# Moving the centering matmul behind the gate products in the projection step of a four-layer triangle kernel

## The chip, the cores and the metric

The kernel runs on one core of one Trainium2 chip. The metric is the device time of one execution in microseconds. Five engines work side by side, each through its own list of instructions in order: TensorE (PE; its weight loads are PEld), VectorE (DVE), ScalarE (ACT), GpSimd (POOL) and SyncE (SP), which issues the transfers. They wait for each other through counting semaphores.

## What is computed

The input `x` has 256 x 256 tokens of 64 channels. Four layers follow each other, and each adds its result to `x`:

```python
x = x + _L0_conv_ref(_gn(x), ...)
x = x + _L1_conv_ref(_gn(x), ...)
x = x + _L2_conv_ref(_gn(x), ...)
x = x + _L3_conv_ref(_gn(x), ...)
```

`_gn` is a group norm. Layers 0, 1 and 3 have one shape; this is layer 0, cut:

```python
xn = layernorm(x, norm_g, norm_b)
left = xn @ Wl.T * m * jax.nn.sigmoid(xn @ Wlg.T)
right = xn @ Wr.T * m * jax.nn.sigmoid(xn @ Wrg.T)
out_gate = jax.nn.sigmoid(xn @ Wog.T)
out = jnp.einsum('bikd,bjkd->bijd', left, right)
out = layernorm(out, out_norm_g, out_norm_b) * out_gate
return out @ Wout.T
```

Layer 3 has no mask `m`. Layer 2 has no layer norm ahead of its projections, and goes through another function.

## The kernel before

Each layer is done in three stages: the projections (everything up to `left`, `right` and `out_gate`, which go to DRAM), the product over `k`, and the output stage. The change is in the projections of layers 0, 1 and 3, in `project` (L418).

Tokens come in chunks of 512, two rows of the 256 x 256 image for each half of the image; the two halves lie on partitions 0 to 63 and 64 to 127. A layer has 64 chunks (`NCH`), and the main loop does one chunk a step, 16 steps (`BODY`) in one turn of a hardware loop. A step `q` works on several chunks at once, at distances that the line with `CENTER` sets:

```python
LOAD, CENTER, VARIANCE, SPLIT, NORM = 16, 14, 13, 5, 4
```

On TensorE a step issues these products, in an order written out by hand in `step` (L573):

- `spread` for chunk q+4 (L549), which puts 1/sqrt(variance) on all partitions,
- `center` for chunk q+14 (L530), a float32 product that takes the mean away and writes the one bank `Z`,
- `heads` for chunk q, row 0 and row 1 (L562), 24 small float16 products. Row 0 writes `PAIR[0]` and row 1 writes `PAIR[1]`. There is one such buffer a row,
- `out_gate` for chunk q (L569 to L571), three float16 products into the bank `GATE`,
- `variance` for chunk q+13 (L541), a float32 product that adds up squares of eight chunks in the bank `VAR`.

`center` and `variance` stop before the others: the last 14 steps of a layer have no `center`, the last 13 no `variance`.

ScalarE does in each step, in this order: `square` for chunk q+14 (L606, L608), two passes over `Z` that store the centred values (`zs`) and their squares (`sq`); `gate_pair` for chunk q, row 0 and row 1 (L625), the sigmoids of the halves of `PAIR[0]` and `PAIR[1]`; in one step of eight also `root` (L613 to L618), a logarithm and an exponential with table loads around them; and the sigmoid of `GATE` (L642), written to `gates`.

VectorE does `norm` for chunk q+4 (L692, L693, L699), which makes the float16 parts `hi` and `lo` that `heads` reads four steps later, and `left_and_right` for chunk q (L712), which multiplies the other half of `PAIR[0]`, then of `PAIR[1]`, by its sigmoids. That is the last read of the pair buffer. In layers 0 and 1 GpSimd then multiplies by the mask (L745, L759). In layer 3 L712 writes `stage` itself.

These waits hold the step together:

```python
pe.wait_ge(pair_read.sem, pair_read(m * 2 + row - 1))      # heads, row of chunk m
pe.wait_ge(c["gate_done"].sem, c["gate_done"](m))          # out_gate
pe.wait_ge(c["sq_done"].sem, c["sq_done"](readers))        # center
act.wait_ge(c["z_done"].sem, c["z_done"](m + 1))           # square
```

The first says that `heads` of a row may start once L712 has read the same row of the chunk before. The third says that `center` may overwrite `Z` once the squares of the chunk before are made.

Of the kernel before, what the change touches and what calls it, by code (L numbers as in the profile page):

```python
# [41 lines left out]
BODY = 2 * SCH  # L42
# [151 lines left out]
class Fold:  # L194
# [42 lines left out]
    def load(self, sp):  # L237
        for dst, src in self.loads:
            sp.dma_start(dst, src).then_inc(self.loaded.sem, 16)
# [178 lines left out]
def project(nc, n, kind, low, HG, x, a, left_right, c, k, ps):  # L418
# [8 lines left out]
    LOAD, CENTER, VARIANCE, SPLIT, NORM = 16, 14, 13, 5, 4  # L427
    masked, gate = kind != "normed", a["gate"]
    with ExitStack() as ctx:
# [31 lines left out]
        def bodies_of(eng, step):  # L461

            with eng.Fori(0, bodies - 1) as i:
                for q in range(BODY):
                    step(i, q, lambda lead: True)
            for q in range(BODY):
                step(bodies - 1, q, lambda lead: q + lead < BODY)
# [54 lines left out]
        @block.tensor  # L522
        def _(pe):
            def center(i, q, bank, readers):

                m = i * BODY + q
                load = c[f"x_in{q % 8 // 2}"]
                pe.wait_ge(load.sem, load(i * 32 + (q // 8 + 1) * 16))
                pe.wait_ge(c["sq_done"].sem, c["sq_done"](readers))
                pe.matmul(bank, k["center"][:], xs[:, q % 8, :], start=True, stop=True).then_inc(c["z_done"].sem, 1)  # L530

            def variance(i, q):

                m = i * BODY + q
                pe.wait_ge(c["sq_done"].sem, c["sq_done"](m + 1))
                at = q % BATCH
                if at == 0:
                    batch = i * (BODY // BATCH) + q // BATCH
                    pe.wait_ge(c["log_done"].sem, c["log_done"](batch))
                w = k["var_w"][:, 2 * (BATCH - 1 - at):2 * (2 * BATCH - 1 - at)]  # L540
                pe.matmul(VAR, w, sq[:, q % 2, :], start=(at == 0), stop=(at == BATCH - 1)).then_inc(c["var_done"].sem, 1)  # L541

            def spread(i, q):

                m = i * BODY + q
                b = q // BATCH
                pe.wait_ge(c["r_split"].sem, c["r_split"](i * (BODY // BATCH) + b + 1))
                pe.wait_ge(c["xn_done"].sem, c["xn_done"](m))
                pe.matmul(R, k["spread"][:, q % BATCH, :], r_terms[:, b % 2, :], start=True, stop=True).then_inc(c["spread_done"].sem, 1)  # L549

            def heads(i, q, row):
                m = i * BODY + q
                if row == 0:
                    pe.wait_ge(c["lo_done"].sem, c["lo_done"](m + 1))

                pe.wait_ge(pair_read.sem, pair_read(m * 2 + row - 1))
                for kb in range(2):
                    at = row * S + kb * P
                    for step, (tokens, part) in enumerate(((hi, 0), (lo, 0), (hi, 1))):
                        for g in range(2):  # L560
                            half = slice(g * C, g * C + C)
                            last = pe.matmul(PAIR[row][:, g, kb * S:kb * S + S], tokens[half, q % 8, at:at + P],  # L562
                                             k["w_heads"][half, part, :], start=(step == 0), stop=(step == 2))
                last.then_inc(c["proj_done"].sem, 1)

            def out_gate(i, q):
                m = i * BODY + q
                pe.wait_ge(c["gate_done"].sem, c["gate_done"](m))
                pe.matmul(GATE, k["w_gate"][:, 0, :], hi[:, q % 8, :], start=True, stop=False)  # L569
                pe.matmul(GATE, k["w_gate"][:, 0, :], lo[:, q % 8, :], start=False, stop=False)  # L570
                pe.matmul(GATE, k["w_gate"][:, 1, :], hi[:, q % 8, :], start=False, stop=True).then_inc(c["gate_mm_done"].sem, 1)  # L571

            def step(i, q, more):  # L573
                if more(NORM):
                    spread(i, q + NORM)
                if more(CENTER):
                    center(i, q + CENTER, Z, i * BODY + q + CENTER)
                heads(i, q, 0)
                heads(i, q, 1)
                out_gate(i, q)  # L580
                if more(VARIANCE):
                    variance(i, q + VARIANCE)

            fold.multiply_statistics(pe)
            pe.wait_ge(fold.done.sem, fold.done(8))

            between = {0: (fold.multiply_bias, fold.center_output), 1: (fold.multiply_weights,), 4: (fold.turn_sizes,),
                       5: (fold.spread_sizes,)}
            for q in range(CENTER):
                center(0, q, AHEAD_Z[q % 2], q - 1)  # L590
                if q > 0:
                    variance(0, q - 1)
                for part in between.get(q, ()):
                    part(pe)
                if q >= CENTER - NORM:
                    spread(0, q - (CENTER - NORM))
            pe.wait_ge(fold.done.sem, fold.done(fold.all_steps))
            bodies_of(pe, step)

        @block.scalar  # L600
# [918 lines left out]
```

## Time and profile before

| | |
|---|---|
| median of 3 runs | 2241.92 us |
| all three | 2240.76, 2241.92, 2245.84 us |
| profiled execution, device time | 2241.74 us |
| its span, first to last instruction | 2239.9 us |
| mean granted TensorE clock | 0.948 |
| PE busy | 1814.5 us (81%) |
| DVE busy | 1521.0 us (68%) |
| ACT busy | 1309.4 us (58%) |
| POOL busy | 807.1 us (36%) |

The device time is 1.8 us above the span of the same execution. Busy shares are means over stages with different limits, so a stage is read by itself. The main loops of the projections lie at about 97 to 372 us (layer 0), 720 to 995 us (layer 1) and 1631 to 1908 us (layer 3). Starts of instructions on one engine tell its pace; matmul records overlap each other, so their durations are not added up.

### The profile page before, as it was taken

The page shows a single profiled execution, that of the slowest core. Times are in us where ns is not written, and L with a number is a line of the kernel's source. Part 1 is how long each engine was busy: PE and PEld are TensorE (multiplying, and loading weights), DVE is VectorE, ACT ScalarE, POOL GpSimd, SP SyncE. Part 2 cuts the span into 40 slices and gives each one's busy share as a digit, 9 for nine tenths or more (in the row PEclk, how much of TensorE's full clock was granted, in tenths as well). Part 3 has the DMA queues.
Part 4 walks back from the last instruction along what each step waited for, and adds up shares of the span by engine and source line. Part 5 has one row for each costly group of instructions (what it writes and reads, how often), then busy time and mean ns, then how long its engine had stood idle before and what let it go on. Part 6 is the DMA issues. An engine that isn't in the chain of part 4 may idle for free. (4 is left out here: it accounts for less than half of the span.)

```text
span 2239.9 us, 40644 instructions
## 1 busy us (share of the span) xinstructions
PE 1814.5 (81%) x10389; PEld 966.6 (43%) x10389; DVE 1521.0 (68%) x3171; ACT 1309.4 (58%) x2413; POOL 807.1 (36%) x740
## 2 busy tenths in 40 slices
PE   0999994897998999955699786777799998499766
PEld 0333442784542344333355464633233434388432
DVE  7588885226745999966875575488488889244675
ACT  0577773466995777744599464333377776144322
POOL 0144444006960444444798000088100000000699
PEclk9999998898999999988899899899899999699999
DMA  7368677775993454547499698399547767655699
GB/s 318 111 189 256 207 240 231 283 293 199 366 335 117 154 183 159 169 142 300 155 366 361 216 305 287 158 365 399 200 127 231 238 212 224 237 230 220 210 352 338
DMA packets 353472, 542.22 MB, mean 242 GB/s; under 512 B 23627, under 2 KB 205518, under 8 KB 345686
## 3 DMA queue, kind: packets, MB, share of 16 engines
q1 hardware_dynamic: 353366, 541.01, 70.1%
q8 instruction: 41, 0.67, 0.1%
q14 instruction: 65, 0.53, 0.1%
HBM read 314.43 MB, written 226.49 MB: 241 GB/s over the span
## 5 line engine op out<-in xcount | busy, mean ns | idle before, releaser
L1263 POOL TENSOR_TENSOR out_scaled<-O,out_rs 128x128 f32<-128x128 f32 (+1 forms) x128 | 97.9, 767 | 739.0 <-DVE out_rs L1170 737.8
L562 PE MATMUL ps<-w_heads,hi 64*128 64x256 f16 x3072 | 292.1, 273 | 29.0 <-DVE sig L712 20.1
L1059 ACT ACTIVATE O<-ps 128x512 f32 (+1 forms) x144 | 151.8, 1054 | 233.4 <-PE ps L979 233.4
L625 ACT ACTIVATE sig<-ps,largest 128x512 f32<-128x512 f32 x384 | 246.5, 691 | 51.4 <-PE ps L562 49.9
L606 ACT ACTIVATE zs<-ps,shift 128x512 f32<-128x512 f32 x192 | 131.7, 686 | 213.3 <-PE ps L530 209.7
L1307 PE MATMUL ps<-ident,out_scaled 128*128 128x128 f32 (+1 forms) x1024 | 163.8, 285 | 107.6 <-POOL out_scaled L1263 107.5
L1307 PEld LDWEIGHTS ps<-ident,out_scaled 128*128 128x128 f32 (+1 forms) x1024 | 114.7, 134 | 278.1 <-POOL out_scaled L1263 193.7
L562 PEld LDWEIGHTS ps<-w_heads,hi 64*128 64x128 f16 x3072 | 154.3, 95 | 181.3 <-issue 65.9
L1004 DVE COPY packed<-right 128x512 f32<-128x512 f32 (+1 forms) x208 | 96.9, 490 | 190.4 <-DMA right<-left_right 141.0
L745 POOL TENSOR_TENSOR stage<-sig,mask 128x512 f32<-128x512 f32 x128 | 133.4, 1076 | 236.2 <-DVE sig L712 236.2
L979 PE MATMUL ps<-left,packed 128*128 128x256 f32 (+1 forms) x768 | 154.7, 355 | 77.8 <-DVE packed L1004 77.0
L562 PE MATMUL ps<-w_heads,lo 64*128 64x256 f16 x1536 | 213.2, 272 | 0.0
L712 DVE SCALAR_TENSOR_TENSOR sig<-ps,largest,sig 128x512 f32<-128x512 f32 x256 | 179.8, 742 | 44.4 <-ACT sig L625 43.0
L759 POOL TENSOR_TENSOR stage<-sig,mask 128x1024 bf16<-128x1024 f32 x64 | 130.4, 2038 | 210.4 <-DVE sig L712 210.4
L530 PE MATMUL ps<-xs,center 128*128 128x512 f32 x384 | 204.6, 615 | 1.1 <-DVE shift L336 1.1
L541 PE MATMUL ps<-sq,var_w 128*16 128x512 f32 x384 | 200.0, 603 | 4.3 <-ACT log_var L615 4.3
L1162 DVE BATCH_NORM_STATS2 out_bn<-O 128x6 f32 (+2 forms) x1024 | 193.8, 255 | 12.5 <-PEq L921 12.3
L1249 POOL TENSOR_TENSOR out_centered<-O,out_bn 128x512 f32<-128x512 f32 x128 | 134.7, 1053 | 149.0 <-DVE out_bn L1162 149.0
L699 DVE TENSOR_TENSOR lo<-xn,hi 128x512 f16<-128x512 f32 x192 | 180.4, 939 | 6.6
L1274 POOL TENSOR_TENSOR out_xo<-out_og,out_xs 128x512 f32<-128x512 f32 x128 | 168.0, 1315 | 28.1 <-DMA x_dram<-out_xo 15.5
L979 PEld LDWEIGHTS ps<-left,packed 128*128 128x128 f32 (+1 forms) x768 | 120.7, 163 | 112.1 <-issue 60.9
L1349 ACT ACTIVATE out_u<-ps 32x512 f32<-32x512 f32 (+1 forms) x128 | 75.5, 590 | 154.1 <-PE ps L1307 154.1
(136 smaller groups left out, 3645.2 us busy)
## 6 DMA issues: line engine op xcount, KB each, us to landing
left_right<-stage SPq DMA_DIRECT2D x128, 512.0 KB, 6.4
out_gs<-gate SPq DMA_DIRECT2D x256, 256.0 KB, 4.5
gate<-gates SPq DMA_DIRECT2D x96, 512.0 KB, 2.9
x_dram<-out_xo SPq DMA_DIRECT2D x192, 256.0 KB, 4.3
out_xs<-x_dram SPq DMA_DIRECT2D x192, 256.0 KB, 4.6
left<-left_right SPq DMA_DIRECT2D x22, 2048.0 KB, 7.8
right<-left_right SPq DMA_DIRECT2D x22, 2048.0 KB, 12.2
xs<-x_dram SPq DMA_DIRECT2D x64, 512.0 KB, 4.1
```

What stands on the lines that cost most here:

```text
L530: pe.matmul(bank, k["center"][:], xs[:, q % 8, :], start=True, stop=True).then_inc(c["z_done"].sem, 1)
L541: pe.matmul(VAR, w, sq[:, q % 2, :], start=(at == 0), stop=(at == BATCH - 1)).then_inc(c["var_done"].sem, 1)
L562: last = pe.matmul(PAIR[row][:, g, kb * S:kb * S + S], tokens[half, q % 8, at:at + P], k["w_heads"][half, part, :], start=(step == 0), sto ...
L625: act.activation(sig[:, slot, :].rearrange("p (c e) -> p c e", c=4), pair(row, 0), ACT.Sigmoid, scale=k["largest"][:, 0:1]).then_inc(c["si ...
L699: dve.tensor_tensor(lo[:, q % 8, :], xn[:, q % 2, :], hi[:, q % 8, :], ALU.subtract).then_inc(c["lo_done"].sem, 1)
L712: dve.scalar_tensor_tensor(dst, pair(row, 1).rearrange("p c (n h) -> p c n h", h=HG), k["largest"][:, 1:2], factor, ALU.mult, ALU.mult).th ...
L979: last = pe.matmul(ps[h % 4 // 2][:, h % 2, jb * S:jb * S + S], stationary, moving, start=(kb == 0), stop=(kb == 1))
L1059: act.activation(o_of(ch), ps[h % 4 // 2][:, h % 2, :].rearrange("p (b g i) -> p b g i", b=2, g=2), ACT.Copy).then_inc(c["o_copied"].sem, 1)
L1162: last = dve.bn_stats(bn[:, b, jb, at:at + 2, :].rearrange("p g s -> p (g s)"), tokens.rearrange("p g h -> p h g"))
L1249: pool.tensor_tensor(centered[:, q % RING], rows[:, :, bass.ds(m * 2 * ROWS, 2 * ROWS), :], per_token(bn[:, :, :, :, 1:2], q), ALU.subtrac ...
L1274: pool.tensor_tensor(xo[:, q % RING, :], og[:, q % RING], xs[:, q % RING, :], ALU.add).then_inc(c["x_new"].sem, 1)
L1307: last = pe.transpose(TURNED[q % 4][:, at:at + P], scaled[:, q % RING, jb, 2 * row:2 * row + 2, :].rearrange("p g h -> p (g h)"), k["ident ...
```

## The change

In a step of the main loop, `center` goes from ahead of `heads` to behind `out_gate`. A wait for `sq_done` with the same target as the one inside `center` is put ahead of `out_gate`. The prologue, which centres the first 14 chunks, is not changed, nor is any other engine's list.

```diff
             def step(i, q, more):
                 if more(NORM):
                     spread(i, q + NORM)
+                heads(i, q, 0)
+                heads(i, q, 1)
+                if more(CENTER):
+                    pe.wait_ge(c["sq_done"].sem, c["sq_done"](i * BODY + q + CENTER))
+                out_gate(i, q)
                 if more(CENTER):
                     center(i, q + CENTER, Z, i * BODY + q + CENTER)
-                heads(i, q, 0)
-                heads(i, q, 1)
-                out_gate(i, q)
                 if more(VARIANCE):
                     variance(i, q + VARIANCE)
```

Two places of the order show it. First TensorE, from the variance product of one step to the first `heads` product of the next. Names in brackets are the semaphores waited for. Before:

```order
L541 MATMUL ps<-sq,var_w 16x512 [waits sq_done]
L548 REGISTER_ALU [waits r_split]
L549 MATMUL ps<-r_terms,spread 128x512 [waits xn_done]
L529 REGISTER_ALU [waits x_in1]
L530 MATMUL ps<-xs,center 128x512 [waits sq_done]
L556 ISA [waits lo_done]
L562 MATMUL ps<-w_heads,hi 128x256 [waits pair_read]
```

The same engine after the change, from the gate products of one step to the first `heads` product of the next:

```order
L569 MATMUL ps<-hi,w_gate 128x512 [waits gate_done,sq_done]
L570 MATMUL ps<-lo,w_gate 128x512
L571 MATMUL ps<-hi,w_gate 128x512
L530 MATMUL ps<-xs,center 128x512 [waits sq_done,x_in1]
L541 MATMUL ps<-sq,var_w 16x512 [waits sq_done]
L548 REGISTER_ALU [waits r_split]
L549 MATMUL ps<-r_terms,spread 128x512 [waits xn_done]
L556 ISA [waits lo_done]
L562 MATMUL ps<-w_heads,hi 128x256 [waits pair_read]
```

The centre product of chunk q+14 now stands behind the gate products of chunk q, and between it and the `heads` of chunk q+1 stand the variance and the spread product. Before, the next products behind the centre were the `heads` of the same step.

Second ScalarE, one step after the change (its line numbers are two higher than before, as two lines were added above):

```order
L608 ACTIVATE zs<-ps,shift 128x512 [waits xn_done,z_done]
L610 ACTIVATE sq<-ps,shift 128x512 [waits var_done]
L625 ISA
L626 REGISTER_ALU [waits proj_done]
L627 ACTIVATE sig<-ps,largest 128x512 [waits lr_done]
L625 REGISTER_ALU
L626 REGISTER_ALU [waits proj_done]
L627 ACTIVATE sig<-ps,largest 128x512 [waits lr_done]
```

Nothing moved here: the two passes over the centre product still stand ahead of the sigmoids of the same step.

## Rows read from the trace of the kernel before

**Rows 1.** The page's busy shares: busy us, share of the span, instructions.

```profile
PE 1814.5 (81%) x10389; PEld 966.6 (43%) x10389; DVE 1521.0 (68%) x3171; ACT 1309.4 (58%) x2413; POOL 807.1 (36%) x740
```

**Rows 2.** Windows: stretch, its length, busy us by engine, PEclk, DMA share, GB/s.

```profile
120.00:140.00 20.00, 20.00 (x157) 8.51 (x155) 16.03 (x24) 14.01 (x24) 9.90 (x10) 1.00 0.53 169
340.00:360.00 20.00, 14.00 (x166) 8.96 (x166) 18.75 (x28) 11.54 (x18) 12.34 (x12) 1.00 0.73 214
962.00:970.00 8.00, 4.77 (x58) 2.92 (x56) 7.93 (x11) 3.92 (x7) 3.93 (x3) 1.00 0.22 88
1880.00:1900.00 20.00, 14.44 (x158) 7.67 (x158) 18.63 (x25) 11.65 (x18) 0.00 (x0) 1.00 0.93 271
```

**Rows 3.** Timeline, one steady step of layer 0: start us, duration us, instruction.

```profile
204.47 0.39 PE L549 MATMUL ps<-r_terms,spread 128*128 128x512 bf16 x1
...
204.69 1.02 PE L530 MATMUL ps<-xs,center 128*128 128x512 f32 x2
...
205.65 0.28 PE L562 MATMUL ps<-w_heads,hi 64*128 64x256 f16 x2
...
205.75 0.69 ACT L606 ACTIVATE zs<-ps,shift 128x512 f32<-128x512 f32 x1 [1.31 <-PE ps L530]
...
206.91 1.26 ACT L625 ACTIVATE sig<-ps,largest 128x512 f32<-128x512 f32 x2
...
207.06 0.39 PE L569 MATMUL ps<-hi,w_gate 128*128 128x512 f16 x1
...
207.63 1.41 DVE L712 SCALAR_TENSOR_TENSOR sig<-ps,largest,sig 128x512 f32<-128x512 f32 x2 [0.72 <-ACT sig L625]
...
207.81 1.03 PE L541 MATMUL ps<-sq,var_w 128*16 128x512 f32 x2
208.05 0.70 ACT L642 ACTIVATE gates<-ps,largest 128x512 f32<-128x512 f32 x1
...
208.78 0.39 PE L549 MATMUL ps<-r_terms,spread 128*128 128x512 bf16 x1
```

**Rows 4.** Timeline, a step of layer 0 without centre and variance.

```profile
343.35 1.40 DVE L712 SCALAR_TENSOR_TENSOR sig<-ps,largest,sig 128x512 f32<-128x512 f32 x2
...
344.24 0.29 PE L562 MATMUL ps<-w_heads,hi 64*128 64x256 f16 x2 [0.98 <-DVE sig L712]
...
345.65 0.39 PE L569 MATMUL ps<-hi,w_gate 128*128 128x512 f16 x1
```

**Rows 5.** Timeline, the same of layer 3.

```profile
1887.71 1.98 DVE L712 SCALAR_TENSOR_TENSOR stage<-ps,largest,sig 128x512 f32<-128x512 f32 x2
...
1890.51 0.39 PE L569 MATMUL ps<-hi,w_gate 128*128 128x512 f16 x1
```

**Rows 6.** Timeline, a step with the root in layer 0, and the next root.

```profile
143.45 1.26 ACT L625 ACTIVATE sig<-ps,largest 128x512 f32<-128x512 f32 x2
...
144.73 1.28 ACT L613 ACT_TABLE_LOAD   x1
...
148.76 0.69 ACT L642 ACTIVATE gates<-ps,largest 128x512 f32<-128x512 f32 x1
...
149.50 0.39 PE L569 MATMUL ps<-hi,w_gate 128*128 128x512 f16 x1 [1.52 <-ACT gates L642]
...
180.81 1.28 ACT L613 ACT_TABLE_LOAD   x1
```

**Rows 7.** Line L625 by itself: its table loads (ns: min, median, max).

```profile
L625 ACT ACT_TABLE_LOAD  x3: 1283/1283/1283, 99.0 to 1632.7; - x3
```

**Rows 8.** Timeline, the root step without a centre in layer 0.

```profile
328.41 0.39 PE L569 MATMUL ps<-hi,w_gate 128*128 128x512 f16 x1 [1.98 <-ACT gates L642]
...
329.62 0.61 PE L549 MATMUL ps<-r_terms,spread 128*128 128x512 bf16 x1 [0.39 <-DVE r_terms L677]
```

**Rows 9.** Windows of one us at both kinds of root step.

```profile
148.00:149.00 1.00, 0.00 (x0) 0.00 (x0) 0.93 (x3) 0.99 (x2) 0.00 (x0) 1.00 1.09 324
...
331.00:332.00 1.00, 1.00 (x14) 0.81 (x12) 1.00 (x3) 0.01 (x1) 1.00 (x2) 0.50 1.09 364
```

## The prediction

> **What bounds the kernel now.** I read the page first: TensorE is busy 81% of the span, more than any other engine [rows 1], but that is a mean over twelve stages. So I cut out the stage that the change touches. In the main loop of the projections TensorE is busy all of a 20 us window at full granted clock (1.00, the 2.4 GHz level), while VectorE has 16.03 us and ScalarE 14.01 us of work [rows 2]. The timeline of one step shows how it is packed. From spread to spread are 4.31 us (204.47 to 208.78), and TensorE starts something new all the time: spread 0.22 us, centre 0.96, heads 1.41, gate products 0.75, variance 0.97 [rows 3]. ScalarE keeps up: it stands idle 1.31 us before each pass over the centre product. It waits for TensorE, not TensorE for it. One step in eight holds the root, and there TensorE waits 1.52 us for the gate sigmoid; eight steps take 36.08 us (144.73 to 180.81) where eight plain ones would take 34.5 [rows 6].
>
> So a step costs what TensorE's instructions cost, and every wait on another engine is covered by other products. The question is whether it stays covered.
>
> **The chain that the change closes.** ScalarE works in order, and its list is not changed: the two passes over centre q+14 come ahead of the sigmoids of chunk q. VectorE's product of row 0 needs the first sigmoid, and the heads of chunk q+1 need that product, since there is one pair buffer a row. Before, the centre was issued ahead of heads q, so the passes ran under heads q. Now the centre comes behind the gate products of chunk q, so heads q+1 wait for: centre, two passes, sigmoid, product. Only variance and spread lie beside that. It is a ring, centre to centre, and its length is:
>
> - centre start to first pass: 204.69 to 205.75, 1.06 us [rows 3]
> - first pass to first sigmoid: 205.75 to 206.91, 1.16 us [rows 3]
> - first sigmoid to VectorE's product: 206.91 to 207.63, 0.72 us [rows 3]
> - product to first heads of the next chunk, where heads wait for it: 343.35 to 344.24, 0.89 us [rows 4]
> - heads to gate products: 344.24 to 345.65, 1.41 us [rows 4]
> - gate products to what follows: 207.06 to 207.81, 0.75 us [rows 3]. What follows was the variance; now it is the centre, whose weights are larger. The three gate products alone take 0.65, so 0.65 to about 0.85 is possible. I take 0.75, from the row where a float32 product follows the same three.
>
> Sum **5.99 us a step** against 4.31. TensorE's own instructions still take 4.31, so it stands idle 1.7 us in each step: variance and spread end their issue 2.15 us after the centre starts (0.96 + 0.97 + 0.22), and the heads may start at 3.83. In layer 1 the product has the same shape. In layer 3 both products are longer, and from the first product to the gate products there are 2.80 us (1887.71 to 1890.51, [rows 5]) in place of 0.89 + 1.41. That makes **6.49 us**.
>
> Not on the ring: the gate sigmoid of chunk q starts 1.14 us after the first sigmoid and takes 0.70 [rows 3], so it is done 4.1 us after the centre, before the next gate products need it at 5.24. VectorE's norm of the next chunk fits between the second product and the next first one; its work, 16.03 us in 20 us or 3.5 us a step, is well under 5.99. The added wait for `sq_done` asks for the squares of chunk q+13, made in the step before; it costs nothing, since those squares stand ahead of the sigmoids that heads waited for. If it were late, the gate products and all behind them would be too, but it cannot be later than the product that released the heads. Loads, stores and GpSimd get the same instructions over a longer time: the transfers take 0.53 of the engines in the first window [rows 2]. They cost nothing more.
>
> **The root steps.** Here the gate sigmoid ends the wait. From the first sigmoid to the gate products of the next step are 6.05 us (143.45 to 149.50, [rows 6]), which holds two table loads, the logarithm and the exponential. The variance that the root reads is done 2 us after the centre, before the root starts. Centre to centre: 1.06 + 1.16 + 6.05 + 0.75 = **9.02 us**, in all three layers. Before, such a step took 4.31 + 1.52 = 5.8.
>
> **The sum.** A layer has 64 - 14 = 50 steps with a centre, so 49 intervals from centre to centre, 6 of them with a root. Before: 6 x 36.08 + 4.31 = 220.8 us. After, layers 0 and 1: 43 x 5.99 + 6 x 9.02 = 311.7; layer 3: 43 x 6.49 + 6 x 9.02 = 333.2. To that come the ends: the first centre starts 1.41 + 0.75 later than before, and from the last centre to the next heads there are 3.83 us in place of 4.31, together +1.7; and the table load for the first sigmoid, 1.28 us [rows 7], was beside TensorE's work and now is in the ring, +1.3. So layers 0 and 1: 311.7 - 220.8 + 3.0 = +94 each; layer 3: 333.2 - 220.8 + 3.0 = +115. **Together +303 us.** The 14 steps behind them are as before.
>
> **The clock** is the term with no row of its own. In a new root step TensorE stands idle from the end of heads (5.2 us, with the tail of the last product 5.3) to the gate products at 8.3, near 2.9 us. What rows show: an idle of 1.52 us in the root steps before leaves the granted clock at 1.00 [rows 6, 9]. In the root step without a centre TensorE stood idle 1.98 us, then again 0.39 us, and the spread product behind it took 0.61 in place of 0.39 us; the clock was 0.50, the 1.2 GHz level [rows 8, 9]. The gap of 2.9 us is on the far side of both, so I take it that the clock falls after each of the 18 roots. Then the parts of the ring that TensorE does are doubled for a while: centre about +1.0, part of the gate products +0.3, and, if it lasts that long, heads +1.4. Bounds 0 (it never falls) and 1.06 + 0.75 + 1.41 = 3.2 us; I take 2.0, nearer the second row. 18 x 2.0 = **+36 us**. In plain steps the idle is 1.7 us of 5.99. The stretches without a centre have the same pattern (TensorE busy 14.00 of 20 us, 4.77 of 8, 14.44 of 20, an idle gap in each step), and their clock is 1.00 [rows 2], so I expect no fall there.
>
> Total +303 + 36 = +339 us on the profiled execution's 2241.7, which stands 0.2 us under the median of the runs: **2581 us**.
>
> The Trainium skill, Perfetto Trace Analysis, section Matmuls, says that independent groups should rotate through PSUM banks, so that ScalarE's and VectorE's reading of one lies under the next group's products. By that rule alone, with rows 0 and 1 in two buffers and `Z` and `GATE` in two more, the move would cost nothing, and the sum would be 0. The 0.98 us that the heads wait in each step without a centre [rows 4] speaks against it: two buffers that are both needed again in the next step don't cover the reading.
>
> **The rivals.**
>
> *The clock falls in every turn.* The new idle comes back in each step, and the third layer's is longer, near 1.9 us (heads may start at 4.16, after 2.15 of issue and a tail of 0.1). If this holds the clock at the lower level, the TensorE parts of the ring double: +3.2 us a step. In layer 3 alone that is 50 x 3.2 = +160, 2740 us; in all three +480, about 3060 us. For it: 1.98 + 0.39 us idle was enough once [rows 8]. Against: the windows at 1.00 with gaps of the same kind [rows 2]. [...] Chance 10%.
>
> *The cover holds, no change* (2242 us). Variance and spread would have to hide passes, sigmoid and product. They give 2.15 us, and 3.83 are wanted; it decides at 1.7 us less of either. Chance 3%.
>
> *Faster, through the root stall.* Heads now stand directly behind spread, 0.96 us earlier in the step. If the sigmoids started that much earlier, the gate sigmoid behind each root would too, and up to 0.96 us of each 1.52 us stall [rows 6] would go: 18 x 0.96 = 17 us, 2224 us. It decides at whether ScalarE can start sigmoid q before centre q+14 is there. Its list says no: the pass stands ahead, and waits. Chance 2%.
>
> **How the numbers follow.** The forecast, with its own bounds, gets 85%. Low end: no fall of the clock and 0.65 for the hand-over, 303 - 15 = +288, 2530 us. High end: 18 x 3.2 = +58 for the roots, 303 + 58 = +361, 2603 us; and I add +47 for layer 3 at the low clock in some 15 of its 50 steps (15 x 3.2), 2650 us. The range 2530 to 2650 leaves out most of the first rival and the two small ones. A measurement of this kernel can tell a change of about 0.2% from none. Slower by more than that has 95%, no change 3%, faster 2%.
>
> **What would show it.** Starts of the centre product 5.99 us apart in layers 0 and 1 and 6.49 in layer 3, 9 to 11 at a root; ScalarE's first pass with its idle before it grown from 1.31 to about 3 us; heads with some 1.5 us idle before them, released by L714 (the product's new line); gate products waiting for the gate sigmoid only at the root; 18 dips of the granted clock to 0.50. The prediction is wrong if heads show no wait in steady steps, if the plain step is not within 0.2 us of these lengths, or if the clock is down in plain steps.

## The result and the profile after

| | before | after |
|---|---|---|
| median | 2241.34 us (4 runs) | 2574.57 us (4 runs) |
| ratio to before, 95% interval | | 1.1481 [1.1463, 1.1499] |
| profiled execution, device time | 2241.74 us | 2567.97 us |
| its span | 2239.9 us | 2566.2 us |

One run after (7906.1 us) and one run of e11 (4708.87 us) were in a slow state and take no part in any ratio; the median of the other three after is 2572.74 us. That is 331.4 us above the median before; 2581 was forecast, between 2530 and 2650. The profiled executions lie 326.3 us apart in span. All line numbers behind the TensorE step are two higher than before, so the product L712 is L714 here and the first pass L606 is L608.

The page after: busy shares, and the granted clock by fortieths of the span.

```profile
PE 1855.1 (72%) x10305; PEld 985.6 (38%) x10389; DVE 1533.2 (60%) x3171; ACT 1311.1 (51%) x2413; POOL 806.4 (31%) x740
...
PEclk9999999798999999997999898998989898989999
...
L562 PE MATMUL ps<-w_heads,hi 64*128 64x256 f16 x3072 | 314.7, 283 | 295.4 <-DVE sig L714 183.6
L608 ACT ACTIVATE zs<-ps,shift 128x512 f32<-128x512 f32 x192 | 131.9, 687 | 537.3 <-PE ps L530 537.3
```

TensorE's share is down from 81% to 72% [rows 1]: the same work in a longer time. The idle ahead of the heads is 295.4 us in all, and nearly all of it ends with VectorE's product (`sig` in layers 0 and 1, `stage` in layer 3). The page before gave 29.0 us for that group. ScalarE waits 537.3 us for the centre product, where it was 213.3.

A steady step of layer 0 after the change, from the timeline (start us, duration us, instruction, idle before it and who ended it). It answers to [rows 3].

```profile
209.69 1.02 PE L530 MATMUL ps<-xs,center 128*128 128x512 f32 x2
210.64 1.03 PE L541 MATMUL ps<-sq,var_w 128*16 128x512 f32 x2
210.75 0.69 ACT L608 ACTIVATE zs<-ps,shift 128x512 f32<-128x512 f32 x1 [2.83 <-PE ps L530]
...
211.91 1.27 ACT L627 ACTIVATE sig<-ps,largest 128x512 f32<-128x512 f32 x2
212.63 1.41 DVE L714 SCALAR_TENSOR_TENSOR sig<-ps,largest,sig 128x512 f32<-128x512 f32 x2 [2.23 <-ACT sig L627]
...
213.44 0.28 PE L562 MATMUL ps<-w_heads,hi 64*128 64x256 f16 x2 [1.76 <-DVE sig L714]
...
214.86 0.39 PE L569 MATMUL ps<-hi,w_gate 128*128 128x512 f16 x1
...
215.52 1.02 PE L530 MATMUL ps<-xs,center 128*128 128x512 f32 x2
```

Centre to centre is 5.83 us in this step. The ring can be read off link by link: centre to first pass 1.06, to the sigmoid 1.16, to the product 0.72, to the next heads 0.81, to the gate products 1.42, to the centre 0.66.

One of these rows has to be read with care. The spread product stands between the variance product and the heads in every step, but its matmul record is missing from this trace in 84 of 192 steps, this one among them (its weight load is there each time, and the page has 84 matmuls fewer than the one before). So the 1.76 us at 213.44 hold 0.32 us of work. Where the record is there, TensorE's idle in a plain step is 1.44 us, as at 219.26 below; in e2, e5 and e8, which keep this ring and lose no such record, it is 1.44 us in nearly every plain step of layers 0 and 1. The spread line by itself after the change (ns: min, median, max, then the first and last start in us):

```profile
L549 PEld LDWEIGHTS ps<-r_terms,spread x192: 95/96/152, 87.9 to 2216.1; 128*128 128x128 bf16 x192
L549 PE MATMUL ps<-r_terms,spread x108: 379/390/634, 90.0 to 2216.4; 128*128 128x512 bf16 x108
```

The step with the root, and the clock behind it: first the timeline, TensorE and the gate sigmoid (it answers to [rows 6]), then windows of one us with the columns of [rows 2].

```profile
219.26 0.28 PE L562 MATMUL ps<-w_heads,hi 64*128 64x256 f16 x2 [1.44 <-DVE sig L714]
...
222.96 0.69 ACT L644 ACTIVATE gates<-ps,largest 128x512 f32<-128x512 f32 x1
...
223.79 0.59 PE L569 MATMUL ps<-hi,w_gate 128*128 128x512 f16 x1 [3.04 <-ACT gates L644]
...
225.03 1.91 PE L530 MATMUL ps<-xs,center 128*128 128x512 f32 x2
```

```profile
222.00:223.00 1.00, 0.00 (x0) 0.00 (x0) 0.96 (x2) 0.99 (x2) 0.00 (x0) 0.88 1.14 340
223.00:224.00 1.00, 0.21 (x1) 0.13 (x2) 0.92 (x4) 0.65 (x1) 0.00 (x0) 0.50 1.06 310
...
228.00:229.00 1.00, 0.76 (x1) 0.10 (x1) 0.07 (x1) 1.00 (x3) 0.00 (x0) 0.50 0.00 0
229.00:230.00 1.00, 0.26 (x6) 0.24 (x8) 1.00 (x2) 1.00 (x2) 0.14 (x1) 0.71 0.00 0
```

TensorE stands idle 3.04 us, the clock falls to 0.50 (1.2 GHz) before the wait is over, and the centre takes 1.91 us in place of 1.02. The windows put the fall at 222.8 and the return at 229.6, 6.8 us later. The same wait does not always end so: in layers 0 and 1 it is 3.04 to 3.12 us at each of twelve roots, and the clock fell at ten of them.

Layer 3 has the same in steps without a root. The timeline shows two plain steps of it, and the windows the clock under the first.

```profile
1914.42 0.28 PE L562 MATMUL ps<-w_heads,hi 64*128 64x256 f16 x2 [1.77 <-DVE stage L714]
...
1916.33 0.61 PE L569 MATMUL ps<-hi,w_gate 128*128 128x512 f16 x1
...
1922.45 0.30 PE L562 MATMUL ps<-w_heads,hi 64*128 64x256 f16 x2 [2.09 <-DVE stage L714]
...
1925.03 0.61 PE L569 MATMUL ps<-hi,w_gate 128*128 128x512 f16 x1
```

```profile
1914.00:1915.00 1.00, 0.58 (x12) 0.50 (x12) 1.00 (x2) 0.40 (x1) 0.00 (x0) 1.00 0.00 0
1915.00:1916.00 1.00, 0.92 (x18) 0.55 (x12) 0.97 (x3) 0.00 (x0) 0.00 (x0) 0.88 0.00 0
1916.00:1917.00 1.00, 1.00 (x6) 0.28 (x3) 0.94 (x2) 0.00 (x0) 0.00 (x0) 0.50 0.00 0
...
1920.00:1921.00 1.00, 0.37 (x1) 0.10 (x1) 0.00 (x0) 1.00 (x3) 0.00 (x0) 1.00 0.04 8
```

Here the heads wait 1.77 us in a step (the 2.09 at 1922.45 hold a spread product whose record is missing), and with a short gap ahead of row 1 TensorE is idle 1.85 us of 6.41. The clock falls in 14 of 43 plain steps.

Read off the starts of ScalarE's first pass, from the one for chunk 14 to the one for chunk 63 in each layer (49 intervals):

| | before | after | plain interval | six root intervals |
|---|---|---|---|---|
| layer 0 | 220.5 us | 313.9 us | 5.82 us | 60.4 us in all, 5 of 6 with a fall of the clock |
| layer 1 | 221.3 | 313.6 | 5.82 | 59.9, 5 of 6 |
| layer 3 | 222.3 | 357.3 | 6.41, but 14 of 43 at 7.75 to 8.13 | 57.9, 3 of 6 |

The growth is 93.4 + 92.4 + 135.0 = 320.8 us of the 326.3 between the two spans. The other 5.5 us lie before, between and behind these stretches, where 5.1 us were forecast for the ends of the loops. Nothing large outside the three loops has to be explained.

### The profile page after: what moved, and what is told of

Same layout as the page of the kernel before. It is cut to its first block and busy times, and to the rows that moved or that the text cites. A ratio compares the mean times of both kernels' runs of the same rounds, so it can differ in the third digit from the quotient of the medians.

```text
span 2566.2 us, 40836 instructions
## 1 busy us (share of the span) xinstructions
PE 1855.1 (72%) x10305; PEld 985.6 (38%) x10389; DVE 1533.2 (60%) x3171; ACT 1311.1 (51%) x2413; POOL 806.4 (31%) x740
## 5 line engine op out<-in xcount | busy, mean ns | idle before, releaser
L562 PE MATMUL ps<-w_heads,hi 64*128 64x256 f16 x3072 | 314.7, 283 | 295.4 <-DVE sig L714 183.6
L608 ACT ACTIVATE zs<-ps,shift 128x512 f32<-128x512 f32 x192 | 131.9, 687 | 537.3 <-PE ps L530 537.3
L1265 POOL TENSOR_TENSOR out_scaled<-O,out_rs 128x128 f32<-128x128 f32 (+1 forms) x128 | 91.7, 718 | 874.4 <-DVE out_rs L1172 873.3
L714 DVE SCALAR_TENSOR_TENSOR sig<-ps,largest,sig 128x512 f32<-128x512 f32 x256 | 180.4, 746 | 235.5 <-ACT sig L627 235.5
L562 PEld LDWEIGHTS ps<-w_heads,hi 64*128 64x128 f16 x3072 | 159.8, 97 | 369.3 <-DVE sig L714 161.0
L714 DVE SCALAR_TENSOR_TENSOR stage<-ps,largest,sig 128x512 f32<-128x512 f32 x128 | 127.6, 1073 | 164.7 <-ACT sig L627 164.7
L530 PE MATMUL ps<-xs,center 128*128 128x512 f32 x384 | 220.0, 657 | 2.3 <-ACT sq L610 1.3
L562 PE MATMUL ps<-w_heads,lo 64*128 64x256 f16 x1536 | 221.4, 281 | 0.0
L701 DVE TENSOR_TENSOR lo<-xn,hi 128x512 f16<-128x512 f32 x192 | 194.4, 1013 | 6.6
L1276 POOL TENSOR_TENSOR out_xo<-out_og,out_xs 128x512 f32<-128x512 f32 x128 | 161.7, 1264 | 28.6 <-DMA x_dram<-out_xo 16.1
```

Of the source, the lines that this page charges most:

```text
L701: dve.tensor_tensor(lo[:, q % 8, :], xn[:, q % 2, :], hi[:, q % 8, :], ALU.subtract).then_inc(c["lo_done"].sem, 1)
L714: dve.scalar_tensor_tensor(dst, pair(row, 1).rearrange("p c (n h) -> p c n h", h=HG), k["largest"][:, 1:2], factor, ALU.mult, ALU.mult).th ...
L1276: pool.tensor_tensor(xo[:, q % RING, :], og[:, q % RING], xs[:, q % RING, :], ALU.add).then_inc(c["x_new"].sem, 1)
```

## The experiments

The theory: the change closes a ring (centre, two passes, sigmoid, product, heads, gate products, centre), because ScalarE's passes stand ahead of the sigmoids of the same step and each row has one pair buffer. Its length sets the step, and the idle in it brings the clock down now and then. The rival: the new place itself is dear on TensorE, by the added wait, by weights that are not loaded ahead, or by the clock alone.

**e1: open the ring on ScalarE.** TensorE's order is that of the change.

```diff
             def step(i, q, more):
                 m = i * BODY + q
-                if more(CENTER):
-                    square(i, q + CENTER, Z)
                 gate_pair(i, q, 0)
                 gate_pair(i, q, 1)
                 root_step(i, q, more)
...
                 act.activation(gates[:, q % 4, :], GATE, ACT.Sigmoid, scale=k["largest"][:, 2:3]).then_inc(c["gate_done"].sem, 1)
+                if more(CENTER):
+                    square(i, q + CENTER, Z)
```

> TensorE as in the change; only ScalarE's list is altered: the two passes over the centre product come last in a step, behind the gate sigmoid. Ring theory: the sigmoids of chunk q no longer stand behind the centre of the same step, so the ring is open and the plain step goes back to TensorE's own 4.31 us; at a root the passes come late and the step may be some 0.7 us longer than the 5.8 of before. In all 2235 to 2265 us. Rival theory (the centre behind the gate products is dear on TensorE itself, by its weights or by the added wait): nothing changes, about 2570 us.

Measured: 2273.13 us, ratio 1.0141 [1.0117, 1.0165]. Of the 331 us some 300 are gone with TensorE's list untouched, so the place of the centre is not dear in itself. But it came out 8 us above the range. The timeline of a root in e1:

```profile
151.65 0.69 ACT L642 ACTIVATE gates<-ps,largest 128x512 f32<-128x512 f32 x1
152.23 0.68 ACT L608 ACTIVATE zs<-ps,shift 128x512 f32<-128x512 f32 x1
...
152.80 0.69 ACT L610 ACTIVATE sq<-ps,shift 128x512 f32<-128x512 f32 x1
...
153.55 0.39 PE L569 MATMUL ps<-hi,w_gate 128*128 128x512 f16 x1 [2.93 <-ACT sq L610]
```

The gate products now wait for the squares behind the root: the added wait for `sq_done`, which costs nothing in the change, decides here. TensorE stands idle 2.93 us in place of 1.52, 1.4 us more at each of 18 roots, 25 us. The clock also fell at seven of the 18, where in the kernel before it fell at none.

**e2: the added wait only once.** The prologue reads chunk 13 in the bank `GATE`, so the first gate products need the wait. The later ones don't.

```diff
-                if more(CENTER):
-                    pe.wait_ge(c["sq_done"].sem, c["sq_done"](i * BODY + q + CENTER))
                 out_gate(i, q)
...
             pe.wait_ge(fold.done.sem, fold.done(fold.all_steps))
+            pe.wait_ge(c["sq_done"].sem, c["sq_done"](CENTER))
             bodies_of(pe, step)
```

> The change, but the wait for sq_done ahead of the gate products stands once ahead of the main loop and not in each step. Ring theory: it never ended a wait, so the time stays at that of the change, within 0.3% of 2572 us, and the plain step at 5.82 us. Rival theory (the wait holds up TensorE in each step, some 0.1 to 0.2 us): 15 to 30 us less. A third: with its own wait the centre's weights are not loaded ahead, and the plain step grows from 5.82 by up to 0.2 us, 30 us more.

Measured: 2572.77 us, ratio to before 1.1485 [1.1465, 1.1504], the change's being 1.1481. The plain interval is 5.82 and 6.41 us as in the change. The wait costs nothing there, as forecast, and neither rival to that is seen. As this is the same ring a second time, it also shows how the falls of the clock repeat: at 12 of 18 roots and in 15 of 43 plain steps of layer 3, against 13 and 14 in the change.

**e3 and e4: shorten the ring from its TensorE end.** In e3 the centre stands between heads and gate products, in e4 between the two rows of heads; the added wait is left out of both.

First e3:

```diff
                 heads(i, q, 0)
                 heads(i, q, 1)
                 if more(CENTER):
-                    pe.wait_ge(c["sq_done"].sem, c["sq_done"](i * BODY + q + CENTER))
-                out_gate(i, q)
-                if more(CENTER):
                     center(i, q + CENTER, Z, i * BODY + q + CENTER)
+                out_gate(i, q)
```

then e4:

```diff
                 heads(i, q, 0)
-                heads(i, q, 1)
                 if more(CENTER):
-                    pe.wait_ge(c["sq_done"].sem, c["sq_done"](i * BODY + q + CENTER))
-                out_gate(i, q)
-                if more(CENTER):
                     center(i, q + CENTER, Z, i * BODY + q + CENTER)
+                heads(i, q, 1)
+                out_gate(i, q)
```

> The centre between heads and the gate products. Ring theory: the ring loses the 0.66 us of the gate products, so 5.16 us a plain step in layers 0 and 1 and 5.75 in layer 3; the root interval goes back to 7.0 us, since the centre no longer waits for the gate sigmoid; no fall of the clock. From centre to centre 43 x 5.16 + 6 x 7.0 = 264 in place of 220.8 us, layer 3 289; in all +155, about 2400 us. Rival (the position alone is dear, not the length of the ring): as the change, 2570, or as before, 2241.

> The centre between heads row 0 and heads row 1. Ring theory: 1.06 + 1.16 + 0.72 + 0.81 + 0.70 = 4.45 us a plain step in layers 0 and 1, 0.33 more in layer 3 (4.78), a hair above TensorE's own 4.31; root interval 7.0. In all about +53, 2295 us. Rival (any centre behind a heads product costs the whole): near 2400 or 2570 us.

Measured: e3 2426.74 us, ratio 1.083 [1.0808, 1.0851]; e4 2324.4 us, ratio 1.0373 [1.035, 1.0396]. Plain intervals of ScalarE's first pass are 5.27 and 5.85 us (layer 3) in e3, and 4.62 and 4.95 in e4, where 5.16, 5.75, 4.45 and 4.78 were expected. The intervals follow the length of the ring, each 0.10 to 0.17 longer than its sum.

Both totals came out above what was expected, by 27 us in e3 (about 2400) and 29 us in e4 (2295). The longer plain steps make 14 and 22 us of that. The first interval of each layer, which the expectations had left out, is 1.4 us longer than a plain one, and 2.7 to 2.9 in two layers of e3: 7 and 4 us. And "no fall of the clock" did not hold in e3: behind six of its roots a step is 1.1 us longer with the clock down, behind two in e4.

For the 0.10 the timeline of e4 has a reason:

```profile
204.50 0.30 PEld L530 LDWEIGHTS ps<-xs,center 128*128 128x128 f32 x2 [0.21 <-issue]
204.51 1.12 PE L530 MATMUL ps<-xs,center 128*128 128x512 f32 x2
...
205.67 0.69 ACT L606 ACTIVATE zs<-ps,shift 128x512 f32<-128x512 f32 x1 [1.61 <-PE ps L530]
```

and the change beside it:

```profile
215.30 0.41 PEld L530 LDWEIGHTS ps<-xs,center 128*128 128x128 f32 x2
215.52 1.02 PE L530 MATMUL ps<-xs,center 128*128 128x512 f32 x2
...
216.58 0.69 ACT L608 ACTIVATE zs<-ps,shift 128x512 f32<-128x512 f32 x1 [2.82 <-PE ps L530]
```

Behind a long gate product the centre's weights are loaded 0.22 us ahead. Behind the small heads products the load is recorded together with the matmul, and the centre lasts 1.12 in place of 1.02 us. So there the centre costs 0.10 more, and ScalarE starts 1.16 in place of 1.06 us after it. It is the same in most steps: 172 of 192 centre products last 1.12 to 1.13 us in e3 and 174 in e4. That the late load is the reason is read from this pattern; a load made to come earlier was not tried. The other 0.07 us in e4 lies between VectorE's product and the centre (1.57 us for 1.51).

**e10: shorten the ring from its ScalarE end.** Only the squares stay ahead of the sigmoids; the other pass comes behind them.

```diff
                 if more(CENTER):
-                    square(i, q + CENTER, Z)
+                    n = i * BODY + q + CENTER
+                    act.wait_ge(c["z_done"].sem, c["z_done"](n + 1))
+                    act.wait_ge(c["var_done"].sem, c["var_done"](n - 1))
+                    act.activation(sq[:, (q + CENTER) % 2, :], Z, ACT.Square, bias=k["shift"][:])
                 gate_pair(i, q, 0)
                 gate_pair(i, q, 1)
+                if more(CENTER):
+                    act.wait_ge(c["xn_done"].sem, c["xn_done"](n - 15))
+                    act.activation(zs[:, (q + CENTER) % 16, :], Z, ACT.Identity, bias=k["shift"][:]).then_inc(c["sq_done"].sem, 1)
```

> The change, but of ScalarE's two passes only the squares stay ahead of the sigmoids; the pass that stores the centred values comes behind them and signals for both. Ring theory: one pass of 0.58 us leaves the ring, so plain steps 5.24 us in layers 0 and 1 and 5.83 in layer 3, root intervals still 9.0 to 10.5. 3 x 43 x 0.58 = 75 us less than the change, and up to 20 more where the shorter idle in layer 3 keeps the clock up: 2477 to 2500 us. Rival (not the length of the ring but the place of the centre sets the time): 2572 us.

Measured: 2475.16 us, ratio 1.1049 [1.1031, 1.1066], with the median of the centre-to-centre intervals 5.25 us in layers 0 and 1 and 5.84 in layer 3. TensorE's list is that of the change. A pass of 0.58 us taken out of the ring takes 0.57 us off every plain step. In layer 3 TensorE is now idle 1.28 us in a plain step, and the clock falls in none of them. The total is 2 us below the expected range of 2477 to 2500: 74 us from the shorter steps and the 21 us of falls in layer 3 make 95 of the 98 us. Shortened from TensorE's side or from ScalarE's, the step follows the sum of the links. A second pair buffer would be the third way to open the ring; it wasn't tried, since all eight banks of PSUM are in use.

**e5 and e8: does the idle bring the clock down, and what does that cost?** Both give TensorE work that changes no value, in a wait that stays. In e5 the row 1 products behind each root are issued four times in a row, in e8 the spread product of layer 3. First e5:

```diff
-                for kb in range(2):
+                for kb in [kb for turn in range(4 if row == 1 and q % BATCH == 3 else 1) for kb in range(2)]:
```

then e8:

```diff
+                for turn in range(3 if kind == "normed" else 0):
+                    pe.matmul(R, k["spread"][:, q % BATCH, :], r_terms[:, b % 2, :], start=True, stop=True)
                 pe.matmul(R, k["spread"][:, q % BATCH, :], r_terms[:, b % 2, :], start=True, stop=True).then_inc(c["spread_done"].sem, 1)
```

> The change, with the twelve heads products of row 1 issued four times in a row (the same values) in the step behind each root, so that TensorE works 2 us of the 2.9 us in which it waits for the gate sigmoid. The work fits in the wait and lies off the ring. If the idle before the gate products is what lets the clock fall there, the 12 to 13 root intervals of 9.6 to 10.5 us come back to 9.0 and the time falls by 16 to 18 us, to about 2556 us, with the clock at 1.00 in the root steps; the falls in plain steps of layer 3 stay. Rival (the clock falls for another reason, or the falls cost nothing): 2572 or more.

> The change, with the spread product of layer 3 issued four times in a row (the same values), so that TensorE's idle ahead of the heads in a plain step of layer 3 falls from 1.9 to 1.25 us; the heads can't start earlier or later for it. If that idle is what makes the clock fall in 15 plain steps of layer 3 (7.8 to 8.1 us in place of 6.41), all plain steps of layer 3 are 6.41 and the time falls by some 20 us, to about 2552 us. Rival (the idle does not decide): 2572 us or, if the added products were on the ring, up to 64 x 0.66 = 42 us more.

Measured: e5 2557.15 us, ratio 1.1403 [1.1385, 1.142]; e8 2552.92 us, ratio 1.1377 [1.1359, 1.1394]. Against the change's 2572.74 that is 16 and 20 us less (17 and 23 by the ratios), and neither interval touches the change's. More work, less time. In e5 the gate products stand as follows:

```profile
221.31 0.38 PE L569 MATMUL ps<-hi,w_gate 128*128 128x512 f16 x1 [1.08 <-ACT gates L644]
...
221.96 1.02 PE L530 MATMUL ps<-xs,center 128*128 128x512 f32 x2
```

The idle is 1.08 in place of 3.04 us, the centre 1.02 us long. All twelve root intervals of layers 0 and 1 are 8.92 to 9.00 us. In layer 3 one of six is still 10.04, and the clock falls in 17 of its 43 plain steps, where it was 14. In e8 every plain interval of layer 3 but the first is 6.40 to 6.49 us, with an idle of 1.20 us in place of 1.85; the clock there still falls at three of six roots. A window of 260 us over layer 3's loop, first the change, then e8:

```profile
1900.00:2160.00 260.00, 179.88 (x1112) 72.83 (x1128) 139.04 (x201) 123.97 (x196) 0.00 (x0) 0.90 0.45 139
```

```profile
1900.00:2160.00 260.00, 201.80 (x1333) 77.67 (x1332) 149.92 (x216) 133.85 (x210) 0.00 (x0) 0.99 0.48 150
```

The clock's mean rises from 0.90 to 0.99.

**e6, e9, e11, e12: is there a better order?** Each root held up the gate products for 1.52 us in the kernel before. e6 keeps the change's TensorE order and ScalarE does sigmoids, gate sigmoid, passes, root. e9 is the kernel before with one step moved:

```diff
                 gate_pair(i, q, 0)
                 gate_pair(i, q, 1)
-                root_step(i, q, more)
...
                 act.activation(gates[:, q % 4, :], GATE, ACT.Sigmoid, scale=k["largest"][:, 2:3]).then_inc(c["gate_done"].sem, 1)
+                root_step(i, q, more)
```

> TensorE as in the change; ScalarE does sigmoids, gate sigmoid, the two passes over the centre product, and last the root. In e1 the gate products waited at each root for the squares behind the root (2.93 us idle in place of 1.52). Here the squares come ahead of the root, so plain steps 4.31 us and a stall of about 1.2 us a root, at the heads, released by the product: 2232 to 2242 us. If the order of the passes were not the cause of e1's 30 us: about 2270 us.

> The kernel before, TensorE's order untouched; only the root on ScalarE goes behind the gate sigmoid of its step. The gate products of the next step then need not wait for the root, and the passes and sigmoids of the next step come about 8.2 us after the step's start, with the heads wanting the product only at 9.8: stall 0 to 0.3 in place of 1.52 us at each root. 18 to 21 roots x 1.3 to 1.5 = 23 to 32 us less than before, 2209 to 2218 us. Rival (the stall only moves to the heads): 2236 to 2241 us.

Measured: e6 2265.36 us, ratio 1.0098 [1.0083, 1.0114]: 8 us under e1, but not under before, and 23 us above the expected range. Plain steps are 4.31 us, so the ring is open. What is left sits at the roots, in the timeline of e6:

```profile
152.13 0.39 PE L549 MATMUL ps<-r_terms,spread 128*128 128x512 bf16 x1 [1.55 <-DVE r_terms L679]
...
153.03 0.28 PE L562 MATMUL ps<-w_heads,hi 64*128 64x256 f16 x2 [0.50 <-DVE sig L714]
```

I had reckoned with the heads' wait alone and overlooked the spread product's: the root now ends later, and VectorE splits its result in 2.6 us before the spread may read it. The two waits are 2.05 us in place of 1.52, which makes 10 us at 18 roots. The clock also fell behind eight of the 18 roots, and the step there is some 1.5 us longer: 12 us more.

e9 measured 2236.54 us, ratio 0.9981 [0.9971, 0.9991]. It is the fastest kernel here, though by 0.2% only, where more than 1% was expected. The stall moved, as the rival had it, and its place in the timeline of e9 is not the heads but the spread product. The idle is 1.11 us in place of 1.52:

```profile
149.96 0.39 PE L549 MATMUL ps<-r_terms,spread 128*128 128x512 bf16 x1 [1.11 <-DVE r_terms L677]
...
150.34 1.41 DVE L712 SCALAR_TENSOR_TENSOR sig<-ps,largest,sig 128x512 f32<-128x512 f32 x2 [0.45 <-ACT sig L625]
```

e11 and e12 are e9 with more room for the split; both edits are shown against e9. First e11:

```diff
-    LOAD, CENTER, VARIANCE, SPLIT, NORM = 16, 14, 13, 5, 4
+    LOAD, CENTER, VARIANCE, SPLIT, NORM = 16, 14, 13, 4, 3
```

then e12:

```diff
-    LOAD, CENTER, VARIANCE, SPLIT, NORM = 16, 14, 13, 5, 4
+    LOAD, CENTER, VARIANCE, SPLIT, NORM = 16, 14, 13, 5, 3
```

> e9 with the spread product and norm three chunks ahead in place of four and the split one step later, so that the spread no longer waits for the split behind a root (1.11 us idle in e9). If that wait was all that was left of the stall: 18 x 1.1 = 20 us less than e9, about 2217 us. If the heads wait for the late sigmoids by the same amount, as the timeline of e9 suggests (product done 1.2 us after the heads' turn): within 4 us of e9, 2233 to 2241 us.

> e9 with the spread product and norm three chunks ahead in place of four, but the split left where it was in VectorE's list. In e11 the split had come to stand right ahead of the product and the spread that wait for it (2.15 us idle), beside 1.05 us at the heads. Here the first wait should go and the second stay: about 1.05 us a root at the heads, released by the product, none at the spread. Against e9 (1.11 us at the spread): the same within 0.3%, 2230 to 2240 us. If the heads' wait were only an echo of the split: 2215 to 2220 us.

e11 measured 2294.14 us (median of five runs), ratio 1.0242 [1.0226, 1.0257], worse than either branch of its expectation. Its timeline shows a wait at the heads and, in the step behind it, the wait at the spread product, grown from 1.11 to 2.15 us:

```profile
194.49 0.28 PE L562 MATMUL ps<-w_heads,hi 64*128 64x256 f16 x2 [1.05 <-DVE sig L712]
...
199.85 0.39 PE L549 MATMUL ps<-r_terms,spread 128*128 128x512 bf16 x1 [2.15 <-DVE r_terms L677]
```

The split had been moved with the spread, and in VectorE's list it now stood right ahead of a product that the heads want. In layer 1 the spread waits even longer, 2.7 to 2.8 us, and the clock fell at five of the 18 roots. e12 leaves it in its place: 2239.42 us, ratio 0.9991 [0.9979, 1.0003], no change against before. The spread's wait is gone, the heads' 1.05 us is there:

```profile
186.31 0.28 PE L562 MATMUL ps<-w_heads,hi 64*128 64x256 f16 x2 [1.05 <-DVE sig L712]
```

Its trace lacks records of the spread product too, but the weight load for it is issued at 184.00, before the split ends at 185.05, so nothing holds it there.

Behind a root ScalarE has two passes, a table load and the sigmoid to do before VectorE's product, and no order tried here makes that fit.

## Why the prediction was right, and where not

- **The ring.** It held, link by link. Measured 5.82 us against 5.99, and 6.41 against 6.49. Two links were too long in the sum. Product to heads was 0.81, not 0.89; gate products to centre 0.66, not 0.75. The first was taken from [rows 4], where the spread product stands ahead of the heads as it does here; why the link is 0.08 longer there is not shown. The second was taken from the variance product, and the change shows the centre's weights loaded under the last gate product. Together 0.17 x 43 in two layers and 0.08 x 43 in the third: 18 us too much.
- **The root interval.** 8.92 to 9.00 us where the clock stayed up, against 9.02.
- **The first step.** The table load was put at +1.3 us a layer. It measured 2.9 to 3.0, since TensorE's idle there (2.86 us) also brought the clock down: 5 us too little in all. In layer 1 of e3 the first interval had no fall, and there it is 1.4 us longer than a plain one.
- **The clock at roots.** Forecast: a fall after each of 18, 2.0 us each, +36. Measured: 13 of 18, together 16 us above 9.0 an interval, 1.2 to 1.3 each. In e5 the filling took 16 us off the root intervals. This term was mis-sized by a factor of two. In the root step shown above the clock was back when the heads came (their products last 0.28 us), so the part I added for them did not come there.
- **The clock in plain steps.** This is the step that failed. I had written that no fall was expected there, by the windows without a centre [rows 2], and that a clock down in plain steps would show the prediction wrong. In layers 0 and 1 the forecast holds. In layer 3 the clock fell in 14 of 43 plain steps, 21 us. e8 took them away by filling the idle, e10 by shortening it to 1.28 us. The first rival was thus true in part, in one layer and in a third of its steps. The idle was near the 1.7 and 1.9 us that I had reckoned: 1.44 us of 5.82 in layers 0 and 1, 1.85 us of 6.41 in layer 3. What I made of it was wrong: a clock of 1.00 in other stretches with gaps did not carry over. Most of those gaps were shorter, 0.98 us [rows 4]. The gaps of layer 1 were longer than those that layers 0 and 1 have now. This is the kernel before, in a step of 4.07 us:

```profile
964.89 0.29 PE L562 MATMUL ps<-w_heads,hi 64*128 64x256 f16 x2 [1.61 <-DVE sig L712]
```

  There TensorE is idle for a larger share of each step than in layer 3 after the change, and in one gap of almost the same length, and the clock stays at 1.00 [rows 2]. So the share of idle does not sort these cases, and of 43 steps of layer 3 that wait the same 1.77 us the clock falls in only 14. What decides is left open.
- **The total.** The two clock terms together came to 37 us, near the 36 forecast, but for another reason than the one given: the roots cost 20 us less, and layer 3's plain steps 21 us more. That they cancel is luck. Of the 18 us too much in the ring the first steps took back 5, so the forecast lies 13 us above the profiled execution and 8 us above the median of 2572.74. In the range, the 47 us for layer 3 at the low clock should read 48 (15 x 3.2), which changes nothing.
- **The rule on banks** (the Trainium skill, Perfetto Trace Analysis, section Matmuls) gave 0 for the change. It missed by 331 us. e1 and e10 show why it doesn't reach, as they change only the order of ScalarE's list and get back 300 and 98 us: the buffers are read under other products only while the reader's own list lets it come to them.
- **Oscillation of the clock.** The Trainium skill, TensorE: Matmul & The Clock Gate, section "HAM oscillation — how this bites in real kernels", tells of a loop with a wait of some 3 to 5 us for a transfer in every turn, after which every turn starts at the low clock. The waits in plain steps here are shorter, and the clock falls in none of the turns of layers 0 and 1 and in a third of those of layer 3. The waits of 3.04 to 3.12 us at the roots come nearest to that loop, and there the clock fell at ten of twelve.
- **No change** and **faster** had 3% and 2%. Neither was seen; ScalarE waited for the centre 2.8 us a step.

## What to carry to other kernels

Before an instruction is moved on one engine, follow its consumer on the next engine and ask what stands behind that consumer in the same list. If one of those things frees a buffer that the first engine wants next, the move closes a ring, and the step becomes the ring's length however idle the engines are. The other lists can be changed to fit the move (e1, e10), and where an idle remains, harmless work in it can keep the clock up (e5, e8). But a stall that comes from the latency of one serial stretch, like the root here, mostly changes its place.

## What was not expected of the hardware

- An idle of 1.44 us of each 5.82 us left TensorE at full clock through layers 0 and 1 (after the first step and outside the roots). An idle of 1.85 us in 6.41 us brought the clock down in 14 of 43 steps. An idle of 1.61 us in 4.07 us, in the kernel before, left it at 1.00.
- The same wait at a root, 3.04 to 3.12 us, brought the clock down ten times of twelve.
- A trace can lack records of single matmuls, 84 spread products here, and the idle shown behind them is then too long. The weight loads were all there.
- More matmuls made the kernel faster: 64 x 3 = 192 more spread products in e8, 20 us less.
- The float32 centre product is 0.10 us longer when it follows the small heads products (1.12 us) than when it follows a 128x512 gate product (1.02 us).
